# Transposing tile 1's second norm on TensorE, and loading the first mask and context from GpSimd's queue

## The chip, the cores and the metric

The kernel runs on one core of one Trainium2 chip. The metric is the device time of one execution in microseconds (us), as the median over runs of the same kernel; smaller is better.

## The reference

```python
def _L0_xattn_ref(hidden_states, memory_tokens, memory_mask):
    scores = jnp.einsum('bsd,bmd->bsm', hidden_states, memory_tokens) * scale
    scores = jnp.where(memory_mask[:, None, :], scores, neg_inf)
    attn = jax.nn.softmax(scores, axis=-1)
    readout = jnp.einsum('bsm,bmd->bsd', attn, memory_tokens)
    ...
def _L0_ffn_ref(x, weight, lora_A, lora_B, router_w):
    base = jnp.einsum('btd,od->bto', x, weight)
    logits = jnp.einsum('btd,ed->bte', x, router_w)
    ...
    Ax = jnp.einsum('nd,erd->ner', x_flat, lora_A)
    expert_out = jnp.einsum('ner,ne,eor->no', Ax, w_dense, lora_B) * SCALING
    return base + expert_out.reshape(B, T, OUT_F)
x = x + _L0_xattn_ref(_layernorm(x, axis=-1), ctx_2048, mask_BxS2_bk0)
x = x + _L0_ffn_ref(_layernorm(x, axis=-1), L0_ffn_weight, L0_ffn_lora_A, L0_ffn_lora_B, L0_ffn_router_w)
```

x is 8 x 1024 x 1024 in float32; the context has 64 rows for each of the 8 batches. There are 8 experts of rank 16, of which a token takes two.

## The kernel before

The 8192 rows are worked off in 64 tiles of 128 rows, 8 tiles for each batch; a tile is written (batch, j). Each engine has its own program, and every wait is a semaphore written out by hand, so the order of the work is the order of the calls in each engine's block. Two stages run at different tiles at the same time.

Stage one of a tile is attention: the first norm's mean and sum of squares on ACT (`norm1_mean`, `norm1_squares`), its root on POOL (`norm1`), scores on TensorE (`pair_scores` for two tiles at once, then `scores`, a transpose), softmax on DVE and ACT, `e_transpose`, `eT_copy` and `readout`. Then DVE adds the readout to x (`add_readout`) and takes the statistics of the second norm (`norm2_stats`), POOL makes its scale and shift (`norm2`), and ACT writes the normed tile xn.

Stage two is the projection of the normed tile, whose transpose it needs. For all tiles but the first, SP moves xn to xq by four DMAs (`exchange`), DVE transposes 32 x 32 blocks (`x2_transposes`), ACT rounds to the high part (`x2T_high`), and DVE subtracts for the low part (`x2T_low`). Every product of base is three matmuls: high by high, high by low, low by high. The 1160 columns are three groups (`base(tile, g, chunks)`); group 0 has the router's and LoRA's columns too, and a second PSUM bank, groups 1 and 2 have one bank each. So group 1 of a tile can't begin before DVE has emptied the group 1 of the tile before (`add_bases`). Router on DVE and ACT, `h_transpose`, and `lora_second` close a tile.

From tile (0, 2) on all engines repeat one step. Ahead of it stands a start written out by hand, in which the 12 parts of the weights arrive, are rounded on ACT (`w_high`) and subtracted on DVE or POOL (`w_low`), and in which tile (0, 0) is transposed on TensorE instead (`first_norm2`, `first_x2_transposes`, `first_x2T_high`, `first_x2T_low`). `warm(n)` issues n matmuls of the identity with no use for the result, into a bank that is free. b_raw, LoRA's second matrix, is loaded into x's fourth slot, so tile (0, 3) of x is loaded only after `b_low`.

The order of TensorE in the start is, in the lines that the change touches:

```python
            for product in range(3):
                first_base(1, product, range(C))
            first_base(2, 0, range(C))
            h_transpose((0, 0))
            first_base(2, 1, range(C))
            pair_scores((0, 2))
            first_base(2, 2, range(HC))
            scores((0, 2))
            first_base(2, 2, range(HC, C))
            for g in range(G):
                lora_second((0, 0), g)
            base((0, 1), 0, range(HC))
```

## Time and profile before

| | us |
|---|---|
| median of 3 runs | 1095.36 (1095.09 to 1095.86) |
| the profiled execution, its own time | 1095.76 |
| its span | 1094.0 |
| PE busy in the span | 1073.1 (98%) |
| DVE, ACT, POOL busy | 786.2, 468.3, 108.5 |

The span is what the hardware profiler recorded from the first to the last instruction; 1.76 us of the execution lie around it. PE is TensorE's matmuls, DVE is VectorE, ACT is ScalarE, POOL is GpSimd, SP is SyncE, and its queue issues most DMAs. The granted clock of TensorE is a share of full speed. Times within a run are counted from the start of the span.

### The profile page before, as it was taken

To read this page: it belongs to the slowest core of one execution; us is meant where nothing else is said; L and a number is where in the kernel's file an instruction comes from. 1 tells how busy PE (TensorE), PEld (TensorE's weight loads), DVE (VectorE), ACT (ScalarE), POOL (GpSimd) and SP (SyncE) were. 2 spreads that over 40 slices of the span, in tenths; PEclk is the share of its full clock that TensorE was granted. 3 is DMA by queue.
4 is the path that set the end of the run, shared out by engine and by line. 5 is a ranking of instruction groups with operands and counts; after the bars stand their busy time and mean duration, and the time that the engine had idled before them with its cause. 6 is when DMAs were issued, how large, how long until landed. Compare 5 with 4: busy or idle time off the path is not lost.

```text
span 1094.0 us, 18322 instructions
## 1 busy us (share of the span) xinstructions
PE 1073.1 (98%) x6232; PEld 1042.2 (95%) x6232; DVE 786.2 (72%) x2049; ACT 468.3 (43%) x956; POOL 108.5 (10%) x279
## 2 busy tenths in 40 slices
PE   8889999999999999999999999999999999999998
PEld 7779999999999999999999999999999999999998
DVE  5867767668677677677777677677776677776763
ACT  5543443443443543443534444434434434435330
POOL 3210010010010010110100100100100100100100
PEclk9999999999999999999999999999999999999999
DMA  8463524643535544444536435445435535345322
GB/s 290 145 163 117 154 82 132 183 130 121 146 84 165 153 118 132 134 121 140 151 103 177 122 98 146 134 144 153 107 104 154 152 126 154 74 138 154 83 73 78
DMA packets 71838, 145.89 MB, mean 133 GB/s; under 512 B 8944, under 2 KB 44912, under 8 KB 71792
## 3 DMA queue, kind: packets, MB, share of 16 engines
q1 hardware_dynamic: 71136, 144.18, 46.0%
q10 hardware_dynamic: 656, 1.18, 0.3%
q8 instruction: 19, 0.31, 0.1%
q14 instruction: 27, 0.22, 0.1%
HBM read 78.74 MB, written 33.55 MB: 103 GB/s over the span
## 4 chain that ended last, share of the span: by engine, by line
DVE 44%; issue 18%; ACT 15%; PE 14%; POOL 6%; DMA 1%; ACTq 1%; POOLq 0%; SPq 0%; DVEq 0%
DVE x2T L735 10%; DVE x L717 7%; DVE stats L723 7%; DVE xT_lo L742 6%; DVE xT_lo L684 6%; ACT xT_hi L473 4%; PE base_ps L888 4%; PE base_ps L890 4%; PE base_ps L889 4%; POOL rstd L405 3%; ACT xT_hi L503 3%; ACT x2T L457 3%; ACT e_all L485 2%; POOL rstd L401 1%; ACT e_split L487 1%
## 5 line engine op out<-in xcount | busy, mean ns | idle before, releaser
L888 PE MATMUL base_ps<-w_hi,xT_hi 128*128 128x388 f32 x1512 | 529.9, 350 | 1.5 <-DVE x L787 0.4
L889 PE MATMUL base_ps<-w_lo,xT_hi 128*128 128x388 f32 x1512 | 511.9, 339 | 0.0
L890 PE MATMUL base_ps<-w_hi,xT_lo 128*128 128x388 f32 x1512 | 511.6, 338 | 0.0
L888 PEld LDWEIGHTS base_ps<-w_hi,xT_hi 128*128 128x128 f32 x1512 | 285.2, 189 | 13.6 <-DVE x L787 3.7
L889 PEld LDWEIGHTS base_ps<-w_lo,xT_hi 128*128 128x128 f32 x1512 | 285.1, 189 | 2.7
L890 PEld LDWEIGHTS base_ps<-w_hi,xT_lo 128*128 128x128 f32 x1512 | 284.2, 188 | 0.0
L497 ACT ACTIVATE xn<-x,shift,rstd 128x1024 f32<-128x1024 f32 x63 | 78.4, 1244 | 312.0 <-POOL shift L408 312.0
L503 ACT CAST xT_hi<-x2T 128x512 fp32r<-128x512 f32 x126 | 72.0, 618 | 130.2 <-DVE x2T L735 130.2
L735 DVE STREAM_TRANSPOSE x2T<-xq 128x512 f32<-128x512 f32 x126 | 126.7, 1081 | 0.5 <-DMA xq<-xn 0.4
L742 DVE TENSOR_TENSOR xT_lo<-x2T,xT_hi 128x512 fp32r<-128x512 f32 x126 | 81.3, 686 | 34.2 <-ACT xT_hi L503 34.2
L405 POOL TENSOR_TENSOR rstd<-var_eps,neg_half 128x1 f32<-128x1 f32 x64 | 35.8, 559 | 693.2 <-DVE var_eps L728 693.2
L717 DVE SCALAR_TENSOR_TENSOR x<-ro_ps,e_scale,x 128x512 f32<-128x512 f32 x128 | 89.7, 742 | 1.4 <-PE ro_ps L949 1.4
L787 DVE TENSOR_TENSOR x<-base_ps,x 128x386 f32<-128x386 f32 (+1 forms) x192 | 86.1, 503 | 3.0 <-PE base_ps L890 2.9
L723 DVE BATCH_NORM_STATS2 stats<-x 128x6 f32<-128x512 f32 x128 | 82.4, 686 | 2.2
L684 DVE TENSOR_TENSOR xT_lo<-xT_raw,xT_hi 128x1024 fp32r<-128x1024 f32 x64 | 77.8, 1219 | 1.1 <-ACT xT_hi L473 1.1
L464 ACT ACTIVATE x2T<-x,neg_mean 128x1024 f32<-128x1024 f32 x63 | 71.7, 1138 | 0.1
L457 ACT ACTIVATE x2T<-x 128x1024 f32<-128x1024 f32 x63 | 65.7, 1043 | 0.0
L473 ACT CAST xT_hi<-xT_raw 128x1024 fp32r<-128x1024 f32 x64 | 64.0, 1047 | 0.0
L694 DVE SCALAR_TENSOR_TENSOR s_part<-ro_ps,rstd,mask_bias 128x64 f32<-128x64 f32 x64 | 18.2, 284 | 63.3 <-POOL rstd L401 34.1
L888 PE MATMUL base_ps<-b_hi,hT_hi 128*128 128x386 f32 (+1 forms) x192 | 61.6, 321 | 0.7 <-DVE b_lo L680 0.7
L913 PE MATMUL s_ps<-xT_hi,ctxT 128*128 128x256 f32 x248 | 61.1, 284 | 0.5 <-DVE xT_lo L684 0.5
L890 PE MATMUL base_ps<-b_hi,hT_lo 128*128 128x386 f32 (+1 forms) x192 | 61.5, 320 | 0.0
(99 smaller groups left out, 1147.7 us busy)
## 6 DMA issues: line engine op xcount, KB each, us to landing
x<-in_x SPq DMA_DIRECT2D x63, 512.0 KB, 3.5
xq<-xn SPq DMA_DIRECT2D x252, 128.0 KB, 3.5
out<-x SPq DMA_DIRECT2D x63, 512.0 KB, 3.9
xT_raw<-in_xT SPq DMA_DIRECT2D x62, 512.0 KB, 5.2
ctx_raw<-in_ctx SPq DMA_DIRECT2D x15, 256.0 KB, 4.9
w_raw<-in_wT SPq DMA_DIRECT2D x8, 386.0 KB, 8.2
ctxT_raw<-in_ctxT SPq DMA_DIRECT2D x7, 256.0 KB, 4.1
w_raw<-in_wT SPq DMA_DIRECT2D x4, 388.0 KB, 10.3
```

The costliest lines, as they stand in the source:

```text
L457: act.activation(junk, xs, ACT.Identity, scale=-1.0 / D, accum_out=neg_mean1[:, :]).then_inc(ln1_step, 1)
L473: act.copy(xT_hi[:, i], xT_raw[:, k, i]).then_inc(xT_hi_done, 1)
L503: act.copy(chunks(xT2_hi[:, tile[1] % 2], i), chunks(x2T, i)).then_inc(x2T_hi_done, 1)
L684: dve.tensor_tensor(xT_lo[:, i], xT_raw[:, tile[1] // 2 % 2, i], xT_hi[:, i].bitcast(f32), ALU.subtract).then_inc(xT_split, 1)
L717: dve.scalar_tensor_tensor(out=xh, in0=half(ro_ps, i), scalar=e_scale[:, :], in1=xh, op0=ALU.mult, op1=ALU.add).then_inc(x1_done, 1)
L723: dve.bn_stats(stats2[:, 6 * i:6 * i + 6], half(x[:, slot(tile), :], i)).then_inc(ln2_step, 1)
L735: dve.transpose(out_[:, i * QS:(i + 1) * QS], xq[:, i * QS:(i + 1) * QS, :].rearrange("p g (c n) -> p g c n", n=QP)).then_inc(x2T_done, 1)
L742: dve.tensor_tensor(chunks(xT2_lo[:, k], i), chunks(x2T, i), chunks(xT2_hi[:, k], i).bitcast(f32), ALU.subtract).then_inc(x2T_split, 1)
L787: dve.tensor_tensor(xg, base_bank(tile, g)[:, 0:n], xg, ALU.add).then_inc(out_done, 1)
L888: pe.matmul(out_, a_hi, w_h, start=start, stop=False, skip_group_check=again)
L889: pe.matmul(out_, a_hi, w_l, start=False, stop=False, skip_group_check=again)
L890: return pe.matmul(out_, a_lo, w_h, start=False, stop=stop, skip_group_check=again)
```

## The change

Six things are changed, all in the start.

1. The mask and both halves of the first batch's context are no longer loaded by SP's and ACT's queues but by GpSimd's, the context after the first half of tile (0, 0)'s transposed x has landed. They have semaphores of their own.
2. ACT makes a small copy of a constant before its first real operation.
3. Tile (0, 1) is transposed on TensorE like tile (0, 0), into the second bank of group 0 and h_ps. Its exchange by four DMAs, its two DVE transposes and its single xn pass on ACT (now two halves) are gone.
4. TensorE works off group 0 of tile (0, 1) before the last product of tile (0, 0) and before `lora_second((0, 0))`.
5. The orders of DVE, ACT and POOL between there and tile (0, 3) are rewritten. One part of the weights, (2, 0), goes from DVE to POOL and (2, 2) from POOL to DVE. POOL does both `norm1` of tiles (0, 2) and (0, 3) ahead of `norm2((0, 2))`.
6. `warm(5)` becomes `warm(6)` in four places.

```diff
+        def first_x2T(tile, i):
+
+            if tile == (0, 0):
+                return base_bank(tile, 1 + i)[:, :]
+            return base_bank(tile, 0)[:, :] if i == 0 else h_ps[:, :]
...
-            load_mask(0)
-            sp.dma_start(ctx_raw[0:M, :], ctx_in[0]).then_inc(ctx_loaded[0], 16)
...
-            exchange((0, 1))
...
+            pool.dma_start(mask_raw[:, :], mask_in[0].partition_broadcast(P)).then_inc(first_ctx_loaded[2], 16)
+            pool.wait_ge(xT_loaded[0][0], 16)
+            pool.dma_start(ctx_raw[0:M, :], ctx_in[0]).then_inc(first_ctx_loaded[0], 16)
+            pool.dma_start(ctx_raw[M:P, :], ctx_in[0]).then_inc(first_ctx_loaded[1], 16)
             norm1((0, 0))
             ctx_low(pool, 0)
...
             norm2((0, 1))
-            pool.wait_ge(w_split[2][1], 1)
-            w_low(pool, 2, 2)
-            for j in range(TPB):
+            pool.wait_ge(x2T_hi_done, 3)
+            w_low(pool, 2, 0)
+            norm1((0, 2))
+            norm1((0, 3))
+            norm2((0, 2))
+            norm2((0, 3))
+            for j in range(2, TPB):
                 step((0, j))
...
-            def first_norm2():
-
-                act.wait_ge(shift2_done, 1)
+            def first_norm2(tile):
+
+                act.wait_ge(shift2_done, count(tile, 1, 1))
+                act.wait_ge(x2T_done, count(tile, TS))
                 for i, done in enumerate([first_xn_half, xn_done]):
                     act.activation(half(xn, i).rearrange("p (c a n) -> p a c n", a=Q, n=QP),
-                                   x[:, 0, :].rearrange("p (a c n) -> p a c n", a=Q, n=QP)[:, :, i * HC:(i + 1) * HC],
+                                   x[:, slot(tile), :].rearrange("p (a c n) -> p a c n", a=Q, n=QP)[:, :, i * HC:(i + 1) * HC],
                                    ACT.Identity, bias=shift2[:, :], scale=rstd2[:, :]).then_inc(done, 1)
...
-            def first_x2T_high():
+            def first_x2T_high(tile):
 
                 for i in range(2):
-                    act.wait_ge(x2T_done, i + 1)
-                    act.copy(chunks(xT2_hi[:, 0], i), base_bank((0, 0), 1 + i)[:, :]).then_inc(x2T_hi_done, 1)
+                    act.wait_ge(x2T_done, count(tile, TS, i + 1))
+                    act.copy(chunks(xT2_hi[:, tile[1]], i), first_x2T(tile, i)).then_inc(x2T_hi_done, 1)
...
-            act.dma_start(ctx_raw[M:P, :], ctx_in[0]).then_inc(ctx_loaded[1], 16)
             act.dma_start(xT_raw[:, 0, 1, HC:C, :], xT_in[1][:, HC:C, :]).then_inc(xT_rest_loaded[1], 16)
+            act.wait_ge(constants_ready, CONSTANTS)
+            act.copy(gate_num[:, :], neg_half[:, :]).then_inc(tables_loaded, 1)
...
             for r in range(3):
                 w_high(2, r)
-            norm2((0, 1))
+            first_norm2((0, 1))
+            w_high(2, 3)
+            first_x2T_high((0, 1))
             gate_exp((0, 0))
-            w_high(2, 3)
             norm1_mean((0, 2))
             norm1_squares((0, 2))
+            sT_copy((0, 2))
             b_high()
+            softmax_exp((0, 2))
             hT_high((0, 0))
-            sT_copy((0, 2))
-            x2T_high((0, 1))
-            softmax_exp((0, 2))
             eT_copy((0, 2))
             gate_exp((0, 1))
             for i in range(2):
                 xT_high((0, 4), i)
-            norm2((0, 2))
             norm1_mean((0, 3))
             norm1_squares((0, 3))
+            norm2((0, 2))
             softmax_exp((0, 3))
             hT_high((0, 1))
...
-                dve.wait_ge(xq_loaded, count(tile, 16 * Q))
+                dve.wait_ge(xq_loaded, count(tile, 16 * Q, -16 * Q))
...
             w_low(dve, 1, 3)
+            for i in range(2):
+                xT_low((0, 2), i)
+            first_x2T_low((0, 1))
             router_top((0, 0))
             router_gate((0, 0))
-            for i in range(2):
-                xT_low((0, 2), i)
-            w_low(dve, 2, 0)
             w_low(dve, 2, 1)
-            dve.wait_ge(ln1_step, count((0, 2), 2, 2))
-            for i in range(TS):
-                x2_transposes((0, 1), i)
+            softmax_scores((0, 2))
+            w_low(dve, 2, 2)
+            softmax_split((0, 2))
             w_low(dve, 2, 3)
             hT_low((0, 0))
             b_low()
-            x2T_low((0, 1))
-            softmax_scores((0, 2))
-            softmax_split((0, 2))
+            add_readout((0, 2))
+            norm2_stats((0, 2))
             add_bases((0, 0))
             router_top((0, 1))
-            add_readout((0, 2))
-            norm2_stats((0, 2))
             router_gate((0, 1))
             softmax_scores((0, 3))
             softmax_split((0, 3))
             hT_low((0, 1))
+            for i in range(2):
+                xT_low((0, 4), i)
             for i in range(TS):
                 x2_transposes((0, 2), i)
             x2T_low((0, 2))
-            for i in range(2):
-                xT_low((0, 4), i)
             add_readout((0, 3))
             norm2_stats((0, 3))
             add_bases((0, 1))
...
-            def first_x2_transposes():
+            def first_x2_transposes(tile):
 
                 for i, done in enumerate([first_xn_half, xn_done]):
-                    pe.wait_ge(done, 1)
+                    pe.wait_ge(done, count(tile, 1, 1))
                     for c in range(HC):
                         k = (i * HC + c) * P
-                        mm = pe.transpose(base_bank((0, 0), 1 + i)[:, c * P:(c + 1) * P], xn[:, k:k + P], ident[:, :])
+                        mm = pe.transpose(first_x2T(tile, i)[:, c * P:(c + 1) * P], xn[:, k:k + P], ident[:, :])
...
             pe.wait_ge(constants_ready, CONSTANTS)
-            warm(5)
+            warm(6)
             ctx_mean(0)
-            warm(5)
+            warm(6)
             pe.wait_ge(ctxT_split, 1)
             first_scores(0)
             warm(1)
             pe.wait_ge(first_sT_copied, 1)
             pe.transpose(st_ps, sT[:, 0:P], ident[:, :]).then_inc(scores_done, 1)
-            warm(5)
+            warm(6)
             e_transpose((0, 0))
             warm(1)
             readout((0, 0))
             first_scores(1)
             warm(2)
             scores((0, 1))
-            warm(5)
-            first_x2_transposes()
+            warm(6)
+            first_x2_transposes((0, 0))
             first_base(0, 0, range(C))
             first_base(0, 1, range(C))
             first_base(0, 2, range(HC))
@@ -1046,26 +1065,28 @@
             readout((0, 1))
             for product in range(3):
                 first_base(1, product, range(C))
-            first_base(2, 0, range(C))
+            for product in range(2):
+                first_base(2, product, range(C))
+            first_x2_transposes((0, 1))
+            pair_scores((0, 2))
+            base((0, 1), 0, range(HC))
+            scores((0, 2))
+            base((0, 1), 0, range(HC, 6))
             h_transpose((0, 0))
-            first_base(2, 1, range(C))
-            pair_scores((0, 2))
-            first_base(2, 2, range(HC))
-            scores((0, 2))
-            first_base(2, 2, range(HC, C))
+            base((0, 1), 0, range(6, C))
+            first_base(2, 2, range(2))
+            e_transpose((0, 2))
+            first_base(2, 2, range(2, C))
+            readout((0, 2))
             for g in range(G):
                 lora_second((0, 0), g)
-            base((0, 1), 0, range(HC))
-            e_transpose((0, 2))
-            base((0, 1), 0, range(HC, C))
-            readout((0, 2))
             base((0, 1), 1, range(C))
             scores((0, 3))
             base((0, 1), 2, range(3))
             h_transpose((0, 1))
-            base((0, 1), 2, range(3, 6))
+            base((0, 1), 2, range(3, 5))
             e_transpose((0, 3))
-            base((0, 1), 2, range(6, C))
+            base((0, 1), 2, range(5, C))
             readout((0, 3))
```

TensorE, at tile (0, 0)'s group 2 (base_ps2_0), before:

```order
L980 MATMUL base_ps2_0<-w_hi,xT2_hi 128x386 x8
L987 MATMUL h_ps<-ident,h 128x128
L980 MATMUL base_ps2_0<-w_hi,xT2_lo 128x386 x8
L913 MATMUL s_ps<-xT_hi,ctxT 128x256
L914 MATMUL s_ps<-xT_lo,ctxT 128x256
```

and in the change:

```order
L999 MATMUL base_ps2_0<-w_hi,xT2_hi 128x386 x8
L999 MATMUL base_ps2_0<-w_hi,xT2_lo 128x386 x8
L942 MATMUL base_ps0_1<-ident,xn 128x128 x4
L942 MATMUL h_ps<-ident,xn 128x128 x4
L932 MATMUL s_ps<-xT_hi,ctxT 128x256
L933 MATMUL s_ps<-xT_lo,ctxT 128x256
```

Two blocks of four transposes of xn come in ahead of the scores of tiles (0, 2) and (0, 3), and the transpose of h leaves.

DVE, at the end of the softmax of tile (0, 2) (e_scale ends it), before:

```order
L710 TENSOR_TENSOR e_scale<-e_inv,any_valid 128x1
L787 TENSOR_TENSOR x<-base_ps0_0,x 128x252
L787 TENSOR_TENSOR x<-base_ps1_0,x 128x386
L787 TENSOR_TENSOR x<-base_ps2_0,x 128x386
L750 MAX top8<-base_ps0_1 128x8
L753 MAX_INDEX top8_at<-top8,base_ps0_1 128x8
L755 CAST top2_at<-top8_at 128x2
```

and in the change, from the last part of the weights on:

```order
L294 TENSOR_TENSOR w_lo<-w_raw0,w_hi 128x2x386
L802 TENSOR_TENSOR hT_lo<-h_ps,hT_hi 128x128
L702 TENSOR_TENSOR b_lo<-x,b_hi 128x1024
L739 SCALAR_TENSOR_TENSOR x<-ro_ps,e_scale,x 128x512 x2
L745 BN_STATS stats2<-x 128x6 x2
L748 BN_AGGR mean_var2<-stats2 128x2
L750 TENSOR_SCALAR var_eps2<-mean_var2 128x1
L751 TENSOR_SCALAR neg_mean2<-mean_var2 128x1
L809 TENSOR_TENSOR x<-base_ps0_0,x 128x252
L809 TENSOR_TENSOR x<-base_ps1_0,x 128x386
L809 TENSOR_TENSOR x<-base_ps2_0,x 128x386
L772 MAX top8<-base_ps0_1 128x8
```

The additions of tile (0, 0)'s results (base_ps0_0, base_ps1_0, base_ps2_0) and the router's maximum (top8) of tile (0, 1) now stand behind b_lo, the readout's addition and the second norm's statistics of tile (0, 2).

ACT, from the gate of tile (0, 1) to the transposed copy of tile (0, 2), before:

```order
L507 ACTIVATE gate_num<-top8 128x1
L473 CAST xT_hi<-xT_raw 128x1024 x2
L497 ACTIVATE xn<-x,shift2,rstd2 128x1024
L457 ACTIVATE x2T,neg_mean1<-x 128x1024
L464 ACTIVATE x2T,sum_sq1<-x,neg_mean1 128x1024
L485 ACTIVATE e_all,e_sum<-s_all,neg_max 128x64
L487 ACTIVATE e_split<-s_all,neg_max 128x64
L512 CAST hT_hi<-h_ps 128x128
L492 CAST eT<-ro_ps 128x128
```

and in the change:

```order
L524 ACTIVATE gate_num<-top8 128x1
L490 CAST xT_hi<-xT_raw 128x1024 x2
L474 ACTIVATE x2T,neg_mean1<-x 128x1024
L481 ACTIVATE x2T,sum_sq1<-x,neg_mean1 128x1024
L514 ACTIVATE xn<-x,shift2,rstd2 128x1024
L502 ACTIVATE e_all,e_sum<-s_all,neg_max 128x64
L504 ACTIVATE e_split<-s_all,neg_max 128x64
L529 CAST hT_hi<-h_ps 128x128
L509 CAST eT<-ro_ps 128x128
```

The second norm of tile (0, 2) (xn) moved behind the two passes of tile (0, 3)'s first norm.

## Rows read from the trace of the kernel before

**Rows 1.** Windows: from:to, length, busy us by engine, granted clock, DMA share, GB/s.

```profile
24.68:48.14 23.46, 19.58 (x104) 16.60 (x105) 20.30 (x40) 15.62 (x26) 9.55 (x9) 1.00 0.57 171
48.14:68.20 20.06, 16.79 (x94) 15.74 (x94) 11.01 (x35) 8.89 (x19) 1.47 (x4) 1.00 0.46 141
68.20:79.01 10.81, 8.79 (x52) 8.26 (x53) 8.60 (x22) 3.91 (x8) 0.93 (x3) 1.00 0.46 120
79.01:1060.00 980.99, 977.47 (x5708) 953.69 (x5709) 719.15 (x1887) 422.69 (x875) 87.62 (x237) 1.00 0.46 131
```

**Rows 2.** Waits of PE, 0 to 100 us: total, times, longest.

```profile
PE ro_ps L939 <- DVE e_split L705: 2.9, 1, 2.9
```

**Rows 3.** Timeline, first 14 us: start, duration, engine, line [idle before <-releaser].

```profile
5.10 1.28 ACT L473 ACT_TABLE_LOAD   x1 [5.10 <-DMA xT_raw<-in_xT]
6.39 1.04 ACT L473 CAST xT_hi<-xT_raw 128x1024 fp32r<-128x1024 f32 x1
...
5.67 0.69 DVE L650 TENSOR_TENSOR ctxT_centred<-ctxT_raw,h_ps 128x512 f32<-128x512 f32 x1 [0.78 <-PE h_ps L895]
7.47 1.23 DVE L684 TENSOR_TENSOR xT_lo<-xT_raw,xT_hi 128x1024 fp32r<-128x1024 f32 x1 [1.12 <-ACT xT_hi L473]
...
9.35 0.48 PE L902 MATMUL s_ps<-xT_hi,ctxT 128*128 128x128 f32 x1 [1.48 <-DVE ctxT L656]
...
11.64 1.04 ACT L445 CAST ctx_hi<-ctx_raw 128x1024 fp32r<-128x1024 f32 x1 [1.36 <-DMA ctx_raw<-in_ctx]
13.07 0.27 ACT L516 COPY sT<-s_ps 128x128 f32<-128x128 f32 x1 [0.38 <-PE s_ps L903]
```

**Rows 4.** Timeline of PE: warm matmuls, the transpose behind them, and later warm ones.

```profile
13.66 2.34 PE L928 MATMUL base_ps<-ident 128*128 128x128 f32 x10
15.89 0.48 PE L939 MATMUL ro_ps<-ident,e_split 128*128 128x128 f32 x1
...
20.85 1.28 PE L928 MATMUL base_ps<-ident 128*128 128x128 f32 x10
```

**Rows 5.** Tile ctx_raw, first 50 us: its two DMAs from issue to landing.

```profile
DMA to landing us min/median/max: 8.0/8.5/9.0
```

**Rows 6.** Timeline: tile (0, 0) transposed on PE, copied by ACT, subtracted by DVE.

```profile
23.26 1.36 PE L923 MATMUL base_ps<-ident,xn 128*128 128x128 f32 x8 [1.13 <-ACT xn L526]
...
23.95 1.29 ACT L534 CAST xT_hi<-base_ps 128x512 fp32r<-128x512 f32 x2
...
24.57 1.40 DVE L675 TENSOR_TENSOR xT_lo<-base_ps,xT_hi 128x512 fp32r<-128x512 f32 x2 [0.44 <-ACT xT_hi L534]
```

**Rows 7.** Timeline: PE's wait for the last weights; ACT's next norm, start and follower.

```profile
37.60 0.62 PE L980 MATMUL base_ps<-w_hi,xT_hi 128*128 128x386 f32 x2 [0.56 <-ACT w_hi L542]
...
37.45 1.06 ACT L457 ACTIVATE x2T<-x 128x1024 f32<-128x1024 f32 x1
...
39.77 1.03 ACT L538 CAST b_hi<-x 128x1024 fp32r<-128x1024 f32 x1
```

**Rows 8.** Timeline of DVE: weights' low part, b_lo, softmax, bases of tile (0, 0).

```profile
44.29 0.94 DVE L286 TENSOR_TENSOR w_lo<-w_raw,w_hi 128x772 fp32r<-128x772 f32 x1
...
45.35 1.20 DVE L680 TENSOR_TENSOR b_lo<-x,b_hi 128x1024 fp32r<-128x1024 f32 x1
...
47.68 0.28 DVE L694 SCALAR_TENSOR_TENSOR s_part<-ro_ps,rstd,mask_bias 128x64 f32<-128x64 f32 x1
...
49.70 1.34 DVE L787 TENSOR_TENSOR x<-base_ps,x 128x252 f32<-128x252 f32 x3
```

**Rows 9.** Timeline: second norm of tile (0, 2), from its readout to its first matmul.

```profile
53.49 1.41 DVE L717 SCALAR_TENSOR_TENSOR x<-ro_ps,e_scale,x 128x512 f32<-128x512 f32 x2
...
56.74 0.14 DVE L762 TENSOR_SCALAR gate_den<-gate_num 128x1 f32<-128x1 f32 x1
57.76 1.24 ACT L497 ACTIVATE xn<-x,shift,rstd 128x1024 f32<-128x1024 f32 x1 [2.56 <-POOL shift L408]
...
68.20 0.41 PE L888 MATMUL base_ps<-w_hi,xT_hi 128*128 128x388 f32 x1 [0.35 <-DVE xT_lo L742]
```

29 lines of the change are left out of this document (19 added, 10 removed).

## The prediction

> **What bounds the kernel now.** I read the stages by windows first [rows 1], columns length and PE busy. From 79.01 us to 1060 PE is busy for 977.47 of 980.99 us: a matmul each 977.47 / 5708 = 0.171 us, and nothing a change of the start can touch. The three windows ahead of it leave PE idle for 3.88, 3.27 and 2.02 us, 9.2 us together. So the change is worth what it does to the moment at which PE gets into its stride, and at most about 9 us plus what the first 24.68 us give. Then the waits: the longest one of PE is 2.9 us, for the softmax of tile (0, 3) [rows 2]. Last the timelines, to follow who is late behind whom; the start is one chain through ACT, DVE, POOL and PE in turn, with PE waiting most of the time, so every term below is a term of that chain and not of PE's work.
>
> **Part 1, the table load.** ACT's table load stands between the landing of x and the first rounding: 5.10 to 6.38, rounding from 6.39 [rows 3]. With the small copy it runs before 5.10, while ACT has nothing else. The rounding moves forward by 1.28 us, but DVE is busy with the centred context until 5.67 + 0.69 = 6.36 and starts the low part at 6.38 instead of 7.47. The path gains 1.09 us: first scores at 8.26. The granted clock is 1.00 in every window, but what runs there tells of the lower of the two levels: ten warm records take 2.34 us at 13.66 and 1.28 us at 20.85 [rows 4]; 1.2 GHz before, 2.4 GHz after. The copy changes nothing of that. The Trainium skill (ScalarE: Activation LUTs, What ACT_TABLE_LOAD costs) puts 1.38 us of draining behind each load of 1.28 us; the row shows the rounding right behind the load, so the trace disagrees. By that rule the gain would be up to 2.66 us here.
>
> **Part 2, warm(6).** Three of the four have cover: PE waited 1.48 us for the scores [rows 3], 1.13 us for the normed tile [rows 6], and for the context's sum. The one ahead of the first softmax transpose has none: the ten records begin at 13.66 and the transpose follows at 15.89 [rows 4], 0.21 to 0.22 us a record. Two more cost 0.43 us; about 0.1 us of it lies beside the softmax. I take +0.33, between 0 and 0.45. Sum so far -1.09 + 0.33 = **-0.76 us** for all that follows.
>
> **Part 3, context and mask on POOL.** ctx_hi stands on ACT in front of the copy of the scores. It ended at 12.68 and the copy began at 13.07 [rows 3]; now the copy is ready to begin at 11.98, so the context must have landed by 10.94 to cost nothing. POOL issues after the first x, near 5.1. Before, such halves took 8.0 to 9.0 us to land [rows 5], behind other loads of the same queue; x itself was there at 5.10, so a load with nothing ahead of it takes under 4.5 us. The two ends are 9.6 and 14.6. I take 11, since the half context no longer stands behind the queue but shares the engines with it: cost 0, with 0 to +3.7 for the range. The mask is issued near 2 and needed near 12.6. POOL itself has nothing else to do before the first norm. The loads left on SP come forward by two issues, and no term of the sum rests on that.
>
> **Part 4, tile (0, 1) on PE.** The last quarter of the third group's weights let PE go on at 37.60 [rows 7]. ACT now writes xn in two halves in front of it (two operations of 512 take 1.29 us, rows 6, one of 1024 1.04 us, rows 3: +0.25) and no gate_exp (-0.15): 37.60 - 0.76 + 0.10 = 36.94. Ten matmuls follow, 1.71 us: the transposes begin at 38.65. From the first transpose to ACT's copy it is 0.69 us, to DVE's subtraction 0.62 more, and DVE takes 1.40 [rows 6]: done at 41.36. The eight transposes are 1.36 us of new work for PE. What is queued behind them is the dear part. DVE has nothing to do from about 36.5 to 40 because its router work for tile (0, 0) stands behind the subtractions, and ACT's gate and its next norm stand behind DVE's router. So ACT starts the norm of tile (0, 2) at 41.8 and ends 39.77 - 37.45 = 2.32 us later [rows 7], at 44.1; it began at 37.45 before. POOL's root takes it to 45.0 (0.9 us, an estimate from the 1.02 us between 56.74 and 57.76 in rows 9).
>
> **Part 5, DVE from 45.0.** The softmax of tile (0, 2) takes 49.70 - 47.68 = 2.02 us, 0.2 more with a part of the weights (0.94) put into its wait for ACT; another part 0.9, hT_lo 0.2 (estimate), b_lo 1.15 [rows 8]: 49.5. Then readout and statistics of tile (0, 2), 56.74 - 53.49 = 3.25 us [rows 9]: 52.7. Only then come the additions of tile (0, 0), 1.34 us for three [rows 8], of which group 1 is free at 53.6. PE has had group 0 of tile (0, 1) as a filler earlier, ends lora_second at 49.5 + 9 x 0.171 = 51.0 and **waits 2.6 us** for that bank. That is the new wait in place of the exchange's.
>
> **Part 6, the second norm of tile (0, 2).** Additions done at 54.05, router's maximum and gate 0.4 (estimate), two roundings of xT 2.0 (1.04 each less their overlap, rows 3), norm of tile (0, 3) 2.32: 58.8. POOL does that tile's root (0.85) before it may do norm2 (1.02): 60.65, against 57.76 before [rows 9], although the statistics were ready 4 us earlier. From xn's start to the first matmul of tile (0, 2) it was 68.20 - 57.76 = 10.44 us (SP's four issues, the landing, DVE, ACT, DVE), unchanged: **71.1, 2.9 us later than before**. PE waits for it for about 4 us, since it has done its other work by 67.
>
> **Part 7, what is given back.** Before, DVE had the two low parts of tile (0, 4), 2.3 us, behind tile (0, 2)'s transpose; now they lie in its wait for the exchange. So the norm of tile (0, 3) is late by 2.9 - 2.3 = 0.6 us only. PE's own work from 68.20 to 79.01 is 8.79 us with 2.02 idle [rows 1]; from 71.1 it ends at 79.7 with no wait. Both say 79.5 to 79.7 where 79.01 was. From there on nothing differs. **Sum: +0.5 us** (+1.3 for parts 4 to 7, -0.76 for 1 and 2): span 1094.5, execution 1095.76 + 0.5 = 1096.3. The profiled execution is 0.4 above the median of the runs; against the median 1095.36 the forecast is **1095.9 us**. About 0.2%, 2.2 us, is what a measurement of this kernel can tell from no change. The terms of the chain may each be off by 0.1 to 0.3 us, some 1 us in all.
>
> **The rivals.**
>
> *PE is fed as meant.* If the additions of tile (0, 0) or the norms on ACT come earlier than I count (a wait that I put in series runs beside another), the 2.9 us wait of PE [rows 2], the 2.02 us of the third window [rows 1] go and no new one comes: -5 us, 1090.4. For it: statistics of tile (0, 2) ready 4 us earlier, no exchange of 5.6 us. Against it: the hard order on DVE and ACT, in which group 1's additions and norm2 stand behind everything named above. Chance 0.12.
>
> *The clock rises earlier.* With PE less idle before 9, the matmuls of 0.21 us from the first scores on could run at 0.11. The 16 scores would save 1.7 us, the records on the path behind them about 1 more, the sixth pair its 0.33: 3 us below the forecast, 1092.9. Against it: PE was busy without a break from 9.35 to 18 and still slow, to the readout's wide matmuls. Chance 0.10. The Trainium skill (TensorE: Matmul & The Clock Gate, Part 1) says that sustained activity releases the clock; no row here shows which activity counts.
>
> *The context is late (slower).* ACT holds the copy of the scores until ctx_hi is done. Each us of landing behind 10.94 is a us for the whole kernel, since no wait behind it has slack; at 14.6 it is +3.7: 1099.6. It decides (over 0.2%) from a landing at 12.6 on. For it: the DMA engines are at their limit from 8 us on, and POOL makes its issues in turn. Against it: a queue of its own, and less in front. Chance 0.14. The Trainium skill (DMA: Bandwidth & Descriptors, Latency and other measured facts) gives GpSimd's path a first byte after about 1 us against 0.6 us; with that 0.4 us the landing would be at 11.4 and the forecast at 1096.4.
>
> *The clock falls in the new wait of 4 us before tile (0, 2).* The longest wait before, 2.9 us, was followed by matmuls at full speed. At the low level 0.171 becomes about 0.34 us; 1.4 us at least (from the first wide matmul to full speed near 18) up to 9 us at half speed cost 0.7 to 4.5: 1096.6 to 1100.4, taken 1098.4. Chance 0.08.
>
> **Numbers.** Forecast 0.56, of which 0.03 falls on either side of the bound; the two fast rivals 0.22, the two slow ones 0.22, of which about a quarter stays inside the bound. Faster 0.24, same 0.56, slower 0.20. The range, 1092.6 to 1098.8, leaves out the first rival and the worst of the third and fourth.
>
> **What would show it.** Right: the table load before 5.1 and the first scores near 8.3; the first softmax transpose near 15.1; PE's transposes of tile (0, 1) near 38.7; a wait of 2.6 us of PE for DVE's additions near 51; norm2 of tile (0, 2) on ACT near 60.6 and PE's first matmul of it near 71.1; PE at 0.171 us a matmul behind 79.6. Wrong: ctx_hi's start behind 11.0; matmuls at 0.11 us before 15; that wait for the additions missing; or half-speed matmuls behind 71.

## The result, and the profile after

The change is slower: 1100.66 us (median of 7 runs, 1099.74 to 1101.83) against 1095.86 (median of 7 runs of the kernel before, 1094.88 to 1097.26), a ratio of 1.0042 with an interval of 1.003 to 1.0054. The forecast was 1095.9 with a range of 1092.6 to 1098.8, and no change the likeliest case; the slower rival, "the context is late", is what happened. (The forecast's +0.5 us stood on 1095.36, the median of the first 3 runs of the kernel before; over 7 runs it is 1095.86.)

The profiled execution took 1101.83 us and spans 1100.0; it is the longest of the seven, 1.2 us above their median. The windows, with the bounds of [rows 1] from 18.40 on (length, busy PE, PEld, DVE, ACT, POOL, granted clock, DMA share, GB/s):

```profile
0.00:9.35 9.35, 6.89 (x36) 6.41 (x37) 3.83 (x7) 5.19 (x7) 2.95 (x20) 1.00 0.81 239
9.35:18.40 9.05, 2.52 (x17) 2.33 (x17) 0.82 (x5) 2.49 (x5) 2.27 (x3) 0.76 1.06 292
18.40:24.68 6.28, 6.26 (x41) 5.77 (x41) 4.61 (x10) 4.17 (x9) 2.72 (x2) 0.81 0.97 354
24.68:48.14 23.46, 20.89 (x123) 18.39 (x121) 17.19 (x39) 16.44 (x27) 10.85 (x10) 1.00 0.46 158
48.14:68.20 20.06, 17.20 (x86) 15.80 (x87) 13.03 (x39) 9.15 (x22) 2.29 (x6) 0.91 0.12 39
68.20:79.01 10.81, 6.69 (x30) 6.21 (x29) 7.72 (x15) 1.14 (x2) 0.23 (x1) 0.84 1.02 291
```

The second window is the new one: PE busy for 2.52 of 9.05 us, at a time when before it had no break. The waits of PE from 0 to 120 us, the three longest, where the longest in [rows 2] was 2.9:

```profile
PE ro_ps L1050 <- ACT sT L533: 6.5, 1, 6.5
PE base_ps L907 <- DVE xT_lo L764: 4.1, 1, 4.1
PE base_ps L907 <- DVE x L809: 2.4, 1, 2.4
```

The two lower ones are those that the prediction announced (about 4, and 2.6). The first was priced at nothing, with up to 3.7 us in the range. Its releaser is ACT's copy of the scores, and the timeline of the first 20 us shows who holds ACT:

```profile
2.64 1.28 ACT L595 ACT_TABLE_LOAD   x1 [2.64 <-issue]
5.09 0.53 POOL L422 DMA_DIRECT2D ctx_raw<-in_ctx  x1 [2.07 <-DMA xT_raw<-in_xT]
5.13 1.04 ACT L490 CAST xT_hi<-xT_raw 128x1024 fp32r<-128x1024 f32 x1 [1.01 <-DMA xT_raw<-in_xT]
5.37 7.47 SPq L322 DMA_DIRECT2D w_raw<-in_wT  x4
...
8.23 0.33 PE L921 MATMUL s_ps<-xT_hi,ctxT 128*128 128x128 f32 x1 [0.36 <-DVE ctxT L678]
8.50 0.27 PE L921 MATMUL s_ps<-xT_hi,ctxT 128*128 128x128 f32 x1
...
15.77 1.04 ACT L462 CAST ctx_hi<-ctx_raw 128x1024 fp32r<-128x1024 f32 x1 [6.08 <-issue]
16.72 0.26 ACT L533 COPY sT<-s_ps 128x128 f32<-128x128 f32 x1
17.03 0.47 PE L1050 MATMUL ro_ps<-ident,sT 128*128 128x128 f32 x1 [6.53 <-ACT sT L533]
17.30 2.77 PE L947 MATMUL base_ps<-ident 128*128 128x128 f32 x12
19.86 0.42 PE L958 MATMUL ro_ps<-ident,e_split 128*128 128x128 f32 x1
```

The scores are there at 10.2, ACT does nothing for 6.08 us, and it rounds the context at 15.77; only then does it copy the scores, 3.65 us later than before [rows 3], although the table load has moved as meant and the first scores come at 8.23. The profile names "issue" as what ended the idle time, but the operation there waits for the context's two halves, and their DMAs say when they came:

```profile
DMA to landing us min/median/max: 9.2/9.7/10.1
```

Issued at 5.09 and 5.61, they landed at 14.3 and 15.7. At the other end of the start, PE's timeline at its waits, behind the last, and at the first matmul of tile (0, 3):

```profile
26.73 1.36 PE L942 MATMUL base_ps<-ident,xn 128*128 128x128 f32 x8 [1.03 <-ACT xn L544]
...
57.76 0.45 PE L907 MATMUL base_ps<-w_hi,xT_hi 128*128 128x386 f32 x1 [2.37 <-DVE x L809]
...
75.06 0.42 PE L907 MATMUL base_ps<-w_hi,xT_hi 128*128 128x388 f32 x1 [4.12 <-DVE xT_lo L764]
...
76.17 0.52 PE L908 MATMUL base_ps<-w_lo,xT_hi 128*128 128x388 f32 x1
76.50 0.53 PE L909 MATMUL base_ps<-w_hi,xT_lo 128*128 128x388 f32 x1
...
80.94 0.28 PE L932 MATMUL s_ps<-xT_hi,ctxT 128*128 128x256 f32 x1
...
94.00 0.34 PE L907 MATMUL base_ps<-w_hi,xT_hi 128*128 128x388 f32 x1
```

where the kernel before had

```profile
88.10 0.34 PE L888 MATMUL base_ps<-w_hi,xT_hi 128*128 128x388 f32 x1
```

The granted clock (its column stands before the last two) around the last wait:

```profile
74.00:76.00 2.00, 0.94 (x4) 0.97 (x5) 1.77 (x3) 0.71 (x2) 0.00 (x0) 0.86 1.01 393
76.00:78.00 2.00, 2.00 (x8) 2.00 (x7) 1.97 (x4) 0.00 (x0) 0.00 (x0) 0.50 1.06 216
```

From 75.53 to 78.44 each matmul takes 0.32 us to the next instead of 0.18: 1.2 GHz. The clock had also fallen behind the wait of 2.4 us (0.59 and 0.55 in the two windows from 58 to 62), ahead of a wait of 4.1 us that could take this loss up. So three things are to be explained: the context, the two later waits, and this fall of the clock.

### The profile page after: what moved, and what is told of

Same layout as the page of the kernel before. It is cut to its first block, busy times and chain, and to the rows that moved or that the text cites. A ratio compares the mean times of both kernels' runs of the same rounds, so it can differ in the third digit from the quotient of the medians.

```text
span 1100.0 us, 18349 instructions
## 1 busy us (share of the span) xinstructions
PE 1074.8 (98%) x6248; PEld 1044.9 (95%) x6248; DVE 784.0 (71%) x2047; ACT 468.9 (43%) x958; POOL 110.5 (10%) x282
## 4 chain that ended last, share of the span: by engine, by line
DVE 42%; issue 17%; PE 17%; ACT 15%; POOL 6%; DMA 2%; ACTq 1%; POOLq 0%; SPq 0%; DVEq 0%
DVE x2T L757 9%; DVE x L739 7%; DVE stats L745 6%; DVE xT_lo L764 6%; DVE xT_lo L706 5%; PE base_ps L907 5%; PE base_ps L909 5%; PE base_ps L908 5%; ACT xT_hi L490 4%; ACT x2T L474 3%; POOL rstd L410 3%; ACT xT_hi L520 3%; ACT e_all L502 2%; POOL rstd L406 1%; ACT e_split L504 1%
## 5 line engine op out<-in xcount | busy, mean ns | idle before, releaser
L908 PE MATMUL base_ps<-b_lo,hT_hi 128*128 128x386 f32 (+1 forms) x192 | 61.1, 318 | 0.0
```

The costliest lines, as they stand in the source:

```text
L908: pe.matmul(out_, a_hi, w_l, start=False, stop=False, skip_group_check=again)
```

## The experiments

All times are compared with runs of the kernel before on the same chip in the same session; its median was 1095.4 to 1096.6 there. The experiments ran on four chips, so two of them are better compared by their ratios than by their medians. Single executions of one kernel differ by 1 to 4.5 us, and part of that is the landing of the context: three traces that share the change's loads and order up to 60 us (the change and the two fills of its wait) have the rounding of the context (ctx_hi) at 14.45, 15.77 and 15.89, and six with it on SP's and ACT's queues and the mask on GpSimd's have it at 10.40 to 12.43. So a position in one trace tells of the landing and of the edit at once. What the order does is read from stretches that begin behind it, in us, from tile (0, 0)'s transposes to the first matmul of tile (0, 2) and on to that of tile (0, 3):

| kernel | to tile (0, 2) | on to tile (0, 3) | both |
|---|---|---|---|
| before | 44.9 | 19.9 | 64.8 |
| the change | 48.3 | 18.9 | 67.3 |
| its order alone | 48.4 | 18.8 | 67.2 |
| its wait filled with 15 matmuls | 48.4 | 17.6 | 66.1 |
| order mended, first step | 43.8 | 17.6 | 61.4 |
| order mended, second step | 42.7 | 18.9 | 61.7 |
| second step, wait filled with 6 | 42.8 | 17.6 | 60.4 |

The change reaches tile (0, 3) 5.9 us later than the kernel before: 3.5 us of it stand at tile (0, 0)'s transposes (26.73 against 23.26), 2.4 come from the order, and of these 1.2 are the fall of the clock behind the last wait (second row against fourth).

### The context

**The context back on the fast queues, all else as changed.**

```diff
 # sync
+            sp.dma_start(ctx_raw[0:M, :], ctx_in[0]).then_inc(first_ctx_loaded[0], 16)
...
 # gpsimd
-            pool.wait_ge(xT_loaded[0][0], 16)
-            pool.dma_start(ctx_raw[0:M, :], ctx_in[0]).then_inc(first_ctx_loaded[0], 16)
-            pool.dma_start(ctx_raw[M:P, :], ctx_in[0]).then_inc(first_ctx_loaded[1], 16)
...
 # scalar
+            act.dma_start(ctx_raw[M:P, :], ctx_in[0]).then_inc(first_ctx_loaded[1], 16)
```

> The changed kernel, with the two halves of the context issued by SP's and ACT's queues again, the mask still by GpSimd's. Theory A (the late context is the loss): the context lands by about 11.5 us instead of 15.7, ACT starts its rounding there, and the whole start comes 4 to 6 us earlier: 1094 to 1097 us. Rival B (the new order behind tile (0, 1) is the loss, the context only a part that other waits would cover): 1099 to 1100.5 us.

Measured: 1096.9 us, ratio 1.001 (1.0 to 1.002). The semaphores are those of the change. Its profile has the context on ACT at 10.40:

```profile
10.40 1.04 ACT L460 CAST ctx_hi<-ctx_raw 128x1024 fp32r<-128x1024 f32 x1 [0.71 <-DMA ctx_raw<-in_ctx]
11.35 0.26 ACT L531 COPY sT<-s_ps 128x128 f32<-128x128 f32 x1
...
DMA to landing us min/median/max: 7.9/8.1/8.2
```

The waits of 4.1 and 2.4 us stay. By the ratios 3.5, by the medians 3.8 of the 4.8 us are the context's; what is left is 1.1 by the ratio and 1.5 by the medians, where the sum for the other parts had +0.5.

**Why is it late? The mask ahead of it in the queue**: the mask moved back to SP, the context stays on GpSimd.

```diff
+            sp.dma_start(mask_raw[:, :], mask_in[0].partition_broadcast(P)).then_inc(first_ctx_loaded[2], 16)
...
-            pool.dma_start(mask_raw[:, :], mask_in[0].partition_broadcast(P)).then_inc(first_ctx_loaded[2], 16)
```

> The changed kernel, with the mask on SP's queue again and the context left on GpSimd's. Theory A1 (the mask's 128 small packets, ahead in the same queue, hold up the context): the context lands within about 6 us of its issue, near 11.5, and the time is 1095 to 1097 us. Theory A2 (the context shares the DMA engines with the weights' loads) or A3 (GpSimd's own path is slow): it lands at 14.5 to 16 as before and the time stays at 1100 to 1101 us.

Measured: 1102.01, ratio 1.005 (1.0033 to 1.0066); landing in 8.4 to 9.3 us, ctx_hi at 15.25, PE's wait 6.2. That is inside the spread of the three traces above, and nothing in the time: the mask isn't it.

**The weights' loads beside it**: SP holds the weights back until the context is there.

```diff
+            sp.wait_ge(first_ctx_loaded[0], 16)
+            sp.wait_ge(first_ctx_loaded[1], 16)
             for r in range(WPARTS):
                 load_w(0, r)
```

> The changed kernel, with SP waiting for both halves of the context before it issues the first weights. Read for the landing of the context above all. A2 (shared engines): the context lands within 4 to 5 us of its issue, near 10. A1 (behind the mask): near 12. A3 (GpSimd's path): still near 15.7. The time: the first weights are issued near 10 instead of 2.6 and are needed near 16, so some us may come back as a wait for weights: 1095 to 1100 us under A2, 1102 or more under A3.

Measured: 1098.56, ratio 1.0022 (1.0013 to 1.0032), with the landing

```profile
DMA to landing us min/median/max: 6.1/6.2/6.4
```

and ctx_hi at 11.85, earlier than in any trace with the context on GpSimd's queue beside the weights. So of the landings of 7.7 to 10.1 us in the three traces above, 2 to 3.5 us come from sharing with the weights. The 6.2 us that are left, for 256 KB, are not the queue's price alone: the last loads of x landed only at 9.5 and 9.8. And the gain didn't all arrive: tile (0, 0)'s transposes came at 24.92, 1.8 us before the change's, with the granted clock at 0.50 from 16 to 24. Sharing hurts both sides. The queues of the change from 10 to 14 us (packets, MB, share of the 16 engines):

```profile
DMA packets 451, 0.87 MB, mean 218 GB/s; under 512 B 46, under 2 KB 356, under 8 KB 451
...
q1 hardware_dynamic: 330, 0.48, 61.1%
q0 software_dynamic: 121, 0.39, 44.8%
```

and of the kernel before in the same stretch:

```profile
DMA packets 913, 1.39 MB, mean 347 GB/s; under 512 B 70, under 2 KB 766, under 8 KB 913
...
q1 hardware_dynamic: 848, 1.28, 94.8%
```

The engines are busy all the time in both, but with GpSimd's packets among the others they move 218 GB/s instead of 347. In that stretch it is 218 to 264 GB/s in all five traces in which GpSimd's queue still carries the context beside the weights, and 333 to 375 in all ten with the context on SP's and ACT's. By 16 us GpSimd's queue is done and the rate is 393 again.

**An earlier issue**: GpSimd doesn't wait for x.

```diff
-            pool.wait_ge(xT_loaded[0][0], 16)
```

> The change, with GpSimd issuing the context right behind the mask instead of waiting for the first half of x's transpose (issue near 2.8 us instead of 5.1). Theory (the queue's landing is stretched by sharing with the weights' loads and is otherwise slow by itself, 6.2 us): the landing takes 8 to 9.5 us from the issue all the same, so it lands near 12 and the time falls by 2 to 2.5 us against the change, to about the kernel before + 2. Rival (the loads that fill the engines are what the context waits for, whenever it is issued): it lands near 15 as before and the time stays that of the change. Rival (an early context pushes the first loads of x and the context's transpose back): the first scores move from 8.2 to 9 or later and half of the gain is given back.

Measured: 1099.72, ratio 1.0035 (1.0021 to 1.0049). Issued at 3.01 and 3.53 it takes 8.7 to 9.6 us, ctx_hi at 13.22 instead of 15.77, the first scores stay at 8.09. The start is 2.6 us earlier in the profile (tile (0, 2) at 72.48) and the span 2.8, but the medians are only 0.9 apart, inside what they can tell. The landing takes as long from an earlier issue.

**All loads as before**, the table, warm(6) and the order as changed.

```diff
+            sp.dma_start(mask_raw[:, :], mask_in[0].partition_broadcast(P)).then_inc(first_ctx_loaded[2], 16)
+            sp.dma_start(ctx_raw[0:M, :], ctx_in[0]).then_inc(first_ctx_loaded[0], 16)
...
+            act.dma_start(ctx_raw[M:P, :], ctx_in[0]).then_inc(first_ctx_loaded[1], 16)
```

> The changed kernel, with mask and context issued by SP and ACT exactly as in the kernel before; the table load, warm(6) and the new order stay. Theory A: context and mask land as before, near 11.6 and 10.3, so ACT's copy of the scores waits for the context's rounding to 12.7 at most; the time is 1095 to 1097 us. Rival B: 1099 to 1100.5 us. Against e1 it prices the mask on GpSimd's queue: if the hole in the DMA engines' work at 6 to 8 us comes back, the landing is up to 1.5 us later than in e1.

Measured: 1098.17, ratio 1.0021 (1.0011 to 1.003), ctx_hi at 11.2, tile (0, 2) at 70.33 against 69.56 with the mask on GpSimd. These 0.8 us are inside the spread of ctx_hi above. The medians are 1.3 us apart, in the same session, and their intervals touch. So the mask on GpSimd's queue may gain about 1 us; that it does, and why, is not shown.

**And the loads alone**, put into the kernel before:

```diff
-            load_mask(0)
-            sp.dma_start(ctx_raw[0:M, :], ctx_in[0]).then_inc(ctx_loaded[0], 16)
...
+            pool.dma_start(mask_raw[:, :], mask_in[0].partition_broadcast(P)).then_inc(first_ctx_loaded[2], 16)
+            pool.wait_ge(xT_loaded[0][0], 16)
+            pool.dma_start(ctx_raw[0:M, :], ctx_in[0]).then_inc(first_ctx_loaded[0], 16)
+            pool.dma_start(ctx_raw[M:P, :], ctx_in[0]).then_inc(first_ctx_loaded[1], 16)
```

> The kernel before with one part of the change: mask and context issued by GpSimd's queue, the context behind the first x. Theory A (late context): it lands near 15.7 us, the copy of the scores begins near 16.7 instead of 13.07, and the time is 3.5 to 4.5 us over the kernel before. Rival: if the other waits of the start cover the context, under 1 us over.

Measured: 1098.7, ratio 1.003 (1.0018 to 1.0041), ctx_hi at 14.81, the copy of the scores at 15.77 instead of 13.07 [rows 3]. The 2.7 us at the copy come back as 2.1 us between the medians, 3.3 by the ratio. That is a little under the 3.5 us expected: the landing was 0.9 us shorter in this trace (8.8, median) than in the change's.

### The table load and warm(6)

**The small copy alone**, in the kernel before.

```diff
+            act.wait_ge(constants_ready, CONSTANTS)
+            act.copy(gate_num[:, :], neg_half[:, :]).then_inc(tables_loaded, 1)
```

> The kernel before with ACT's small copy ahead of its first rounding alone, nothing else. Part 1's theory (the table load lies on the path): the first scores begin near 8.26 us instead of 9.35, the context is unchanged, so ACT's copy of the scores is held by ctx_hi: the context landed near 11.6 and ctx_hi ends near 12.7, so that only part of the gain survives: 0.4 of 1.09 us (sT at 12.7 instead of 13.07), and the time is 0.2 to 0.6 us below the kernel before, within what can be measured. Rival (the whole gain survives, because the context lands earlier too): sT near 12.0 and 1.1 us less. Rival (an earlier start of PE releases the clock earlier): matmuls at 0.11 us from the first scores on, and 2 us less or more. Rival (the load is followed by a drain): more than 1.1 us of gain at the first rounding.

Measured: 1095.92, ratio 0.9997 (0.9988 to 1.0006). The first scores come at 8.14, the copy of the scores at 12.19, tile (0, 0)'s transposes at 21.74 instead of 23.26 [rows 6]: 1.5 us gained by then. It is lost between 45 and 50 us, from the second LoRA product on, whose matmuls ran at 0.17 to 0.19 us before:

```profile
45.53 0.33 PE L891 MATMUL base_ps<-b_hi,hT_hi 128*128 128x386 f32 x1
45.70 0.45 PE L892 MATMUL base_ps<-b_lo,hT_hi 128*128 128x386 f32 x1
45.95 0.53 PE L893 MATMUL base_ps<-b_hi,hT_lo 128*128 128x386 f32 x1
...
48.21 0.53 PE L891 MATMUL base_ps<-w_hi,xT_hi 128*128 128x388 f32 x1
...
49.73 0.34 PE L891 MATMUL base_ps<-w_hi,xT_hi 128*128 128x388 f32 x1
```

PE had short waits of the same lengths (0.9 and 0.7 us, as before) ahead of both, but here the clock fell behind them, to 0.50 from 46 to 48. The matmul at 49.73 stands at the same time in both traces. In the profiled executions a fall of the clock ate the whole gain. That it does so in every execution was not seen, but the medians agree with it.

**warm(5) in the first experiment's kernel:**

```diff
-            warm(6)
+            warm(5)
```

> The change with the context's halves issued by SP's and ACT's queues (as in the first experiment), and with warm(5) in place of warm(6) in the four places. Part 2's theory (one of the four has no cover, 2 matmuls of 0.11 to 0.21 us): 0.2 to 0.4 us faster than that experiment, too little to be told from it, ratio to the kernel before 1.000 to 1.001; the same waits of PE behind 40 us (2.4 and 4.1). Rival (the sixth pair is what lifts the clock early): the first scores run at 0.21 us a matmul instead of 0.11 and the time is 1.5 to 3 us above that experiment.

Measured: 1097.62, ratio 1.002 (1.0011 to 1.0029), 0.7 us above the first experiment, and the intervals overlap. But the first scores run at the low level. PE's timeline of this run, two of the first scores (between them stands one more record), and under it the same two of the first experiment:

```profile
8.03 0.47 PE L920 MATMUL s_ps<-xT_hi,ctxT 128*128 128x128 f32 x1 [0.49 <-DVE ctxT L677]
8.51 0.41 PE L920 MATMUL s_ps<-xT_hi,ctxT 128*128 128x128 f32 x1
```

```profile
7.91 0.33 PE L920 MATMUL s_ps<-xT_hi,ctxT 128*128 128x128 f32 x1 [1.14 <-DVE ctxT L677]
8.19 0.27 PE L920 MATMUL s_ps<-xT_hi,ctxT 128*128 128x128 f32 x1
```

All five profiles with warm(5) have these two 0.48 to 0.49 us apart, all twelve with warm(6) 0.27 or 0.28. So the sixth pair, and not the earlier table load, brings the high level forward. It is worth little, since the context holds the next step, and the wait for it lets the clock fall again (0.50 from 14 to 20 us in the change).

### The order

**The order alone**: the kernel before with parts 4 to 7 of the prediction, its own loads, table load and warm(5).

```diff
-            norm2((0, 1))
+            first_norm2((0, 1))
+            w_high(2, 3)
+            first_x2T_high((0, 1))
...
+            first_x2_transposes((0, 1))
+            pair_scores((0, 2))
+            base((0, 1), 0, range(HC))
```

> The kernel before with the new order alone: tile (0, 1) transposed on TensorE and the orders of all engines rewritten, but the loads, the table load and warm(5) as before. By the working of the prediction +1.3 us; with the fall of the clock in the wait of 4 us ahead of tile (0, 2) (12 matmuls at 0.32 us instead of 0.17, 1.8 us) about +2.5 us, less what the start gives back behind it. Rival (the new order is a gain once the context is early): 1 us or more below the kernel before.

Measured: 1097.84, ratio 1.0015 (1.0005 to 1.0025). Its waits:

```profile
PE base_ps L904 <- DVE xT_lo L761: 4.1, 1, 4.1
PE base_ps L904 <- DVE x L806: 2.4, 1, 2.4
```

Tile (0, 2)'s first matmul is at 71.10, where the prediction put it (71.1), part of it by luck, since this kernel has neither the table load's gain nor warm(6). The order by itself costs 1.2 to 1.7 us, against +1.3. The last two waits are there without any of the new loads.

**The order mended, first step**, on the first experiment's kernel: POOL's `norm2((0, 2))` in front of `norm1((0, 3))`, ACT's xn pass of tile (0, 2) in front of the gate and the squares, and on DVE the additions before the statistics.

```diff
-            norm1((0, 3))
             norm2((0, 2))
+            norm1((0, 3))
...
-            norm2_stats((0, 2))
             add_bases((0, 0))
+            norm2_stats((0, 2))
```

> e1 (context on SP's and ACT's queues) with three places of the order changed: POOL does norm2 of tile (0, 2) before norm1 of tile (0, 3); ACT does the roundings of xT and the mean of tile (0, 3), then norm2 of tile (0, 2), then the gate; DVE adds tile (0, 0)'s results before the statistics of tile (0, 2). If the two new waits of PE (2.4 us for the additions, 4.1 us for the second norm) are what the order costs, both fall below 1 us, the clock doesn't fall ahead of tile (0, 2), and the time is 4 to 5.5 us below e1: 1091.5 to 1093. If they only make room for another wait, within 1.5 us of e1.

Measured: 1092.07, ratio 0.9954 (0.9938 to 0.9971), 4.8 us below the first experiment by the medians and 6.1 by the ratios. The waits of 4.1 and 2.4 are 1.9 and 0.5, and from tile (0, 0)'s transposes to tile (0, 3) it takes 61.4 us instead of 67.3.

**Second step**: the router of tile (0, 0) in front of tile (0, 1)'s low parts on DVE, and its gate and tile (0, 2)'s mean in front of the high parts on ACT.

```diff
-            first_x2T_low((0, 1))
             router_top((0, 0))
             router_gate((0, 0))
             w_low(dve, 2, 1)
+            first_x2T_low((0, 1))
```

> f1, and DVE does the router of tile (0, 0) and one part of the weights while it waits for the transposes of tile (0, 1), ACT its gate and the mean of tile (0, 2) likewise. DVE's 3.2 us of idle there are filled, and the norm of tile (0, 2) ends about 2 us earlier. If that norm is on the path, another 1 to 2 us below f1; if PE is the bound there by then, the same as f1.

Measured: 1090.93, ratio 0.9948 (0.9932 to 0.9965): 5.7 us faster than the kernel before, and the fastest of all that were timed with it. That it beats the first step is not shown: their intervals overlap, with 4 runs each. Behind tile (0, 0)'s transposes it is 1.0 us shorter to tile (0, 2), but the clock fell behind the wait there (0.62 and 0.52 from 64 to 68), and at tile (0, 3) the two are level, 61.7 and 61.4. Those transposes began at 23.93 in the trace of the first step and at 21.09 in this one (ctx_hi at 12.43 and 10.74), which is most of the difference in where tile (0, 2) begins. Its first matmul is at 63.82, against 67.70:

```profile
63.82 0.42 PE L906 MATMUL base_ps<-w_hi,xT_hi 128*128 128x388 f32 x1 [1.87 <-DVE xT_lo L763]
```

### The fall of the clock behind the wait

**The 4.1 us wait filled**, in the change itself:

```diff
+            pe.wait_ge(out_done, count((0, 2), G, FREE - len(base_ps[0]) * G + 1))
+            for _ in range(32):
+                pe.matmul(base_bank((0, 2), 0)[:, 0:P], ident[:, :], ident[:, :], start=True, stop=True)
             for j in range(2, TPB):
```

> The change, with 32 matmuls of the identity (0.107 us each at the high level, 3.4 us) into the free bank of tile (0, 2)'s group 0, in TensorE's wait of 4.1 us ahead of that tile's first matmul. Theory (the wait itself is what pulls the clock down behind it, and that costs time of its own): the first matmul of tile (0, 2) still begins near 75.1, the matmuls behind it run at 0.18 us instead of 0.32 and the granted clock is 1.00 from 70 to 80; the scores of tile (0, 4) come 1.8 us earlier (83.2 instead of 85.0), the median is 1.5 to 2 us below the change's, ratio to the kernel before 1.002 to 1.003. Rival (the clock falls all the same, since such small matmuls don't hold it): no change against the change, 1.0042. Rival (what is gained is lost behind it, because DVE's or the next exchange's work is what tile (0, 3) waits for): matmuls at full speed behind 75, but a new wait of 1 to 2 us before 95 and the time of the change.

Measured: 1118.07, ratio 1.0204 (1.019 to 1.0218), which no theory had. Two things happened. A matmul of the identity leaves two records on the trace, so the fill took 7.1 us instead of 3.4 and held tile (0, 2) back to 76.64. And in the repeated steps, far behind, PE waited for its own instructions:

```profile
PE base_ps L907 <- issue: 11.4, 5, 2.4
...
q8 instruction: 64, 1.05, 0.4%
```

In every other profile of this study that queue moved 19 packets, and there is no such wait. The five waits stand 134 to 136 us apart, behind 310 us, and behind three of them the granted clock fell too (0.50 to 0.53 in one window of 2 us each). Ahead of the first this trace was within 0.2 us of the change's, so nearly all the 16 us that it is longer stand at these five places. **15 instead of 32:**

```diff
-            for _ in range(32):
+            for _ in range(15):
```

> The fill of the change's 4.1 us wait again, now with 15 matmuls of the identity. The run before showed that each leaves two records of 0.107 us on the trace, so 32 took 6.8 us and held tile (0, 2) back by 2.9 us; 15 take 3.2 us and leave 0.9 us of wait. Theory (the clock's fall behind the wait costs 1.5 us of its own: in the run before it was 4.35 us from tile (0, 2)'s first matmul to the scores of tile (0, 4), in the change 5.88): those two are 4.4 us apart, the granted clock is 1.00 behind the wait, and the median is 1 to 2 us below the change's, ratio 1.002 to 1.0035. And the 11.4 us that PE waited for its own instructions in the repeated steps of the run before (with 64 more records' worth of code) are gone, as in the version that had 26 more. Rival (the clock falls all the same with 0.9 us of wait left): 5.9 us apart and 1.0042. Rival (any code added there moves the loop's fetch): waits of 2.3 us for issue behind 110 us, and 1105 or more.

Measured: 1100.24, ratio 1.0033 (1.0021 to 1.0045), 19 packets again and no wait for issue. The clock holds:

```profile
75.86 0.41 PE L907 MATMUL base_ps<-w_hi,xT_hi 128*128 128x388 f32 x1 [0.82 <-DVE xT_lo L764]
...
80.19 0.28 PE L932 MATMUL s_ps<-xT_hi,ctxT 128*128 128x256 f32 x1
```

4.33 us from the one to the other instead of 5.88: the fall costs 1.55 us at its place and 1.3 up to tile (0, 3), 17.6 us against 18.9. The loop behind keeps that: this trace began 0.7 us later at tile (0, 0)'s transposes and its span is 0.5 us shorter. In the medians 0.4 us are seen (1100.24 against 1100.66; ratio 1.0033 against 1.0042, overlapping), so the gain is shown in the trace and not in the time.

**The same in the fastest version**, with 13 and with 6 matmuls in its 1.9 us wait:

```diff
+            for _ in range(13):
+                pe.matmul(base_bank((0, 2), 0)[:, 0:P], ident[:, :], ident[:, :], start=True, stop=True)
```

> The fastest version so far (router first), with 13 matmuls of the identity (1.4 us) in the wait of 1.9 us ahead of tile (0, 2)'s first matmul, into its free bank. By the theory of the clock the nine to twelve matmuls at half speed behind 64.4 become full ones: 1 to 1.7 us less, 1089.3 to 1090.0, ratio to the kernel before 0.993 to 0.994. Rival (the clock isn't held by them, or a wait behind takes the gain): 1090.5 to 1091, 0.995.

> The fastest version with its 1.9 us wait filled by 6 matmuls of the identity (12 records, 1.3 us) instead of 13 (2.8 us, which held tile (0, 2) back by 0.9 us). Theory: tile (0, 2)'s first matmul is no later than in the version without a fill (63.8), the 5.9 us from it to the scores of tile (0, 4) become 4.4, the median 1089.0 to 1089.6, ratio 0.993 to 0.9942. Rival (over-filled or not makes no difference, since DVE's chain sets what follows): 1089.8 to 1090.2.

Measured: 1089.96 and 1090.08, ratios 0.9941 (0.9927 to 0.9955) and 0.9947 (0.9933 to 0.996), against 0.9948 without. The clock stayed at 1.00 behind the wait in both, and 4.34 us lie between the two marks instead of 5.88, but the time can't be told from the version without a fill. Up to tile (0, 3) the trace with 6 is 1.2 us shorter than the one without (60.4 against 61.7).

## Why the prediction was wrong

The step of the sum that failed is in part 3: "I take 11, since the half context no longer stands behind the queue but shares the engines with it: cost 0". The landing was at 15.7, 4.7 us later. It was beyond even the outer end of 14.6, which had been taken from 9.0 us for a load of SP's or ACT's queue [rows 5]; on GpSimd's queue it took 9.2 to 10.1 us here. (In another trace with the same loads it took 7.7 to 8.8, and ctx_hi began at 14.45, just inside that end.) The reason given, a queue of its own with less in front, counted sharing as the cheap case. The runs on the context show 6.1 to 6.4 us on this queue with the weights held back and 7.7 to 10.1 with them, and that with the context back on the other queues 3.5 to 3.8 of the 4.8 us are gone. A second term was left out of the sum: the fall of the clock behind the wait of 4.1 us, 1.3 us at tile (0, 3). The 0.4 us more to the first byte, which the prediction quoted for GpSimd's path from the Trainium skill (DMA: Bandwidth & Descriptors, Latency and other measured facts), is no measure of that. The evidence against was in the prediction's own rival: the DMA engines are at their limit from 8 us on. Why GpSimd's queue lands later in the same crowd stays open.

The miss can be followed along the path, forecast against trace: first softmax transpose 15.1, 19.86 (+4.8); tile (0, 0)'s transposes 22.5, 26.73 (+4.2); group 1's bank 53.6, 57.76 (+4.2); norm2 of tile (0, 2) 60.65, 64.56 (+3.9); its first matmul 71.1, 75.06 (+4.0). The error is made once, at the beginning, and carried. The rest of the 5.5 us between the spans (1100.0 against 1094.5), 1.5 us, comes behind 75, and 1.3 of it is the clock's. All this is the profiled execution; the median missed by 4.8.

Point by point:

- **Part 1** right at its place (8.26 forecast, 8.23 and 8.14 measured), the rounding behind the load as the rows had it. The Trainium skill (ScalarE: Activation LUTs, What ACT_TABLE_LOAD costs) adds 1.38 us of draining to each switch of tables, and doesn't say on which side of the load. The prediction read it as behind; the traces show it on neither side of this first load (in the change ACT's last issue ends at 2.60, the load runs from 2.64 to 3.92, and the small copy begins at 3.93). Wrong as a term of the sum: alone it gave nothing (0.9997).
- **Part 2** right in the change: the softmax was ready at 19.48 and the transpose came at 19.86, +0.4. The premise that the level stays low until the readout was wrong; the rival "the clock rises earlier" came true for the first scores, by the sixth pair, without its 3 us, because the context held the next step.
- **Parts 4 to 6** right, to a few tenths: from tile (0, 0)'s transposes to tile (0, 2)'s first matmul it was 48.33 us, forecast 71.1 - 22.5 = 48.6; the waits were 2.4 and 4.1, forecast 2.6 and about 4.
- **Part 7** wrong by the clock alone. It gave back 2.3 us between tile (0, 2) and the tile behind; the change gave back 1.0 (18.9 us against the kernel before's 19.9), and with the clock held by the fill 2.3 (17.6). The rival "the clock falls in the new wait" came true beside the first, taken at 0.7 to 4.5 us and worth 1.55 at its place. (A slip beside it: from 71.1, 8.79 us of PE's work end at 79.9 and not at 79.7.)
- The forecast treated its rivals as alternatives. Three came true together.
- "PE is fed as meant" fell by its own counter-argument, and f1 and f2, the two mended orders, show that it was the order: with the second norm and the additions in front, and the context on SP's and ACT's queues in both, they give -5.0 and -5.7 us by the ratios (0.9954 and 0.9948), where that rival had -5. f1 differs from the first experiment (+1.1 us) by the order alone.

## What to carry to other kernels

A transfer put on another queue doesn't leave the queue's competition: take its landing from a row of that queue beside the same loads, or keep the case in which it is slower than the old one as the middle, not as the end. An engine that works in order turns such a landing into everybody's wait, so look at what stands behind the waiting instruction. Where a landing varies from execution to execution, compare stretches that begin behind it. When an operation is moved to make room for the next stage, put the one on which the next tile's chain hangs (here the second norm) in front of all that only fills time.
